# Two attentions written out unit by unit, with row maxima, their transfers and the stores of sums by halves of the queries

## The reference

```python
# biased: 16 heads of 8, a bias by distance added to the scores, no mask
att = jnp.einsum('bhqd,bhkd->bhqk', q, k) * (1.0 / math.sqrt(HS))
att = att + compute_bias(rel_emb, t, t)
att = jax.nn.softmax(att, axis=-1)
o = jnp.einsum('bhqk,bhkd->bhqd', att, v)
# causal: the same sizes, a mask in place of the bias
scores = jnp.where(causal, jnp.einsum("bhqd,bhkd->bhqk", q, k), neg)
attn = jax.nn.softmax(scores, axis=-1)
ctx = jnp.einsum("bhqk,bhkd->bhqd", attn, v)
```

## Time and profile before

| what | value |
|---|---|
| three runs, median (lowest to highest) | 2156.62 us (2148.72 to 2158.24) |
| the profiled execution, and its span | 2163.23 us, 2161.4 us |
| TensorE, VectorE, ScalarE, GpSimd busy, all of the span | 1726.3, 1528.8, 1183.4, 845.2 us |
| biased attention, first turn to last copy | 511 to 1224 us |
| causal attention, first turn to last copy | 1321 to 1831 us |

### The profile page before, as it was taken

One profiled execution on the slowest core, in us unless ns is written; L12 is line 12 of the kernel. 1 busy time (PEld: TensorE's weight loads), 2 busy tenths in 40 slices (PEclk: granted clock), 3 DMA queues, 4 the chain that ended last, 5 costly groups with the idle time before them and its releaser, 6 DMA issues. The chain is left out here.

```text
span 2161.4 us, 44387 instructions
## 1 busy us (share of the span) xinstructions
PE 1726.3 (80%) x14756; PEld 776.0 (36%) x14756; DVE 1528.8 (71%) x2661; ACT 1183.4 (55%) x2278; POOL 845.2 (39%) x1066
## 2 busy tenths in 40 slices
PE   5799999987899989989998536988988887600992
PEld 2666666652122222222222223333333332500772
DVE  4768888878899989989897177776777772570224
ACT  3222222232689878878888533676676776300332
POOL 1100000024477777777777533121111221156354
PEclk8799999997799999999999867898899997555996
DMA  2193000004001001001100315111111110401444
GB/s 77 60 138 78 0 0 0 0 12 140 15 21 35 19 20 37 19 20 27 28 19 5 79 26 154 27 37 24 33 37 37 35 24 14 126 33 55 124 138 139
DMA packets 93747, 103.32 MB, mean 48 GB/s; under 512 B 27137, under 2 KB 61649, under 8 KB 93041
## 3 DMA queue, kind: packets, MB, share of 16 engines
q1 hardware_dynamic: 89456, 92.33, 17.6%
q0 software_dynamic: 4096, 8.43, 1.1%
HBM read 63.65 MB, written 36.80 MB: 46 GB/s over the span
## 5 line engine op out<-in xcount | busy, mean ns | idle before, releaser
L1178 DVE TENSOR_REDUCE ba_at_top<-ps 128x2 f32<-128x1024 f32 x512 | 592.8, 1219 | 36.3 <-PE ps L1078 30.9
L1215 ACT ACTIVATE ba_at_ring<-ps 128x512 f32<-128x512 f32 x1024 | 556.6, 596 | 98.2 <-PE ps L1104 86.3
L1262 POOL TENSOR_TENSOR ba_at_ring<-ba_at_ring,rb_near 128x256 f32<-128x256 f32 (+2 forms) x640 | 480.0, 783 | 199.0 <-ACT ba_at_ring L1215 198.6
L1178 DVE TENSOR_REDUCE ca_at_top<-ps 128x2 f32<-128x1024 f32 (+3 forms) x384 | 352.7, 955 | 86.3 <-PE ps L1078 42.5
L1215 ACT ACTIVATE ca_at_ring<-ps 128x512 f32<-128x512 f32 (+3 forms) x768 | 335.5, 490 | 132.0 <-PE ps L1104 123.1
L1078 PE MATMUL ps<-kop,qop 48*128 48x512 bf16 (+3 forms) x1792 | 345.4, 386 | 65.4 <-DVE ba_at_top L1178 31.1
L1104 PE MATMUL ps<-qop,kop 49*128 49x512 bf16 (+3 forms) x1792 | 343.7, 380 | 60.5 <-DMA qop<-ca_at_negm 14.3
L1123 PE MATMUL ps<-ba_at_ring,ba_at_low 128*32 128x256 f32 (+2 forms) x4096 | 339.4, 405 | 18.1 <-ACT ba_at_osb L1200 15.6
L1104 PEld LDWEIGHTS ps<-qop,kop 49*128 49x128 bf16 x1792 | 86.7, 93 | 442.0 <-ACT ba_at_ring L1215 245.7
L1255 POOL TENSOR_SCALAR_AFFINE_SELECT ca_at_ring<-ca_at_ring 128x512 f32<-128x512 f32 x128 | 81.3, 636 | 417.5 <-ACT ca_at_ring L1215 417.5
L520 ACT ACTIVATE gm_sg<-ps,gm_bias 128x512 f32<-128x512 f32 x128 | 88.0, 687 | 236.3 <-PE ps L460 236.3
(11 more groups left out here) (316 smaller groups left out, 1696.3 us busy)
## 6 DMA issues: line engine op xcount, KB each, us to landing
cs_fc<-in_fc_w SPq DMA_DIRECT2D x32, 256.0 KB, 2.8
qk_parts<-ba_at_ring SPq DMA_DIRECT2D x24, 256.0 KB, 3.6
qop<-qk_parts SPq DMA_DIRECT2D x64, 96.0 KB
kop<-qk_parts SPq DMA_DIRECT2D x64, 96.0 KB
qk_parts<-ca_at_ring SPq DMA_DIRECT2D x24, 256.0 KB, 3.6
ex_xi<-expert_rows_in SPq DMA_DIRECT2D x16, 258.0 KB, 3.1
expert_rows_in<-gm_zero SPq DMA_DIRECT2D x1, 4096.0 KB
expert_rows_out<-gm_zero SPq DMA_DIRECT2D x1, 4096.0 KB
```

The source lines that it names most:

```text
L1178: nc.vector.tensor_reduce(top[:, k0 // CH, 2 * pair:2 * pair + 2, i], k.ps[:, slot:slot + 2, 0:k1 - k0], AX.X, ALU.max).then_inc(a_read, 1)
L1215: nc.scalar.activation(ring[:, t % RING, 0:q1 - q0], k.ps[:, B_BANK + bank_of(g, t), 0:q1 - q0], ACT.Exp).then_inc(exped, 1)
L1262: ins = nc.gpsimd.tensor_tensor(w, w, a.near[:, g * HG + j, lo - (i - 1) * P:hi - (i - 1) * P], ALU.mult)
```

## The change

Only `attend` is changed, for both attentions.

- The loop over batches is gone: all 16 units are written out on every engine, with constant semaphore targets.
- Row maxima are found by halves of the queries: first query tiles 0 to 3 (biased: 16 turns; causal: 8), then tiles 4 to 7 (16 each). Each half has its own join (causal: the second alone), transposition of 16 rows, negation, four DMAs of 4 x 128 elements, and a semaphore `mrow[g][half]`. The scores of a half wait for that half alone.
- All turns and transpositions of all units form one list, ITEMS. A transposition stands two turns behind the last turn of its half. `plan` gives each item a step, ahead of its use by a lead: the larger of two shares (first half's part of the turns; second half's part of the steps) plus AHEAD, 0.2 (biased) or 0.28 (causal). That makes 0.70 of a unit in the biased attention and 0.99 in the causal one. Before step 0 only unit 0's first half is worked off.
- The sums are stored by halves, each with its own semaphore; ScalarE's copy waits for the store of the same half a unit earlier.
- SyncE goes through the steps in one list: loads at step 0 of a unit, `largest` at the step of the transposition, `store` at fixed steps, and `invert` at step 6 of the last unit.

```diff
-    AHEAD = 0.17
-    GAP = 3
+    AHEAD = 0.28 if causal else 0.2
...
-    TILES = [0, 7, 1, 6, 2, 5, 3, 4]
+    TILES = ([0, 1, 2, 3], [4, 5, 6, 7])
...
+        for u in range(NU):
+            for half in range(2):
+                for t in turns_of(half):
+                    push((u, half, t))
+                due.append([2, (u, half, None)])
...
+        lead = max(sum(cost[:n0]) / sum(cost), 1 - begin1) + AHEAD
...
+                when = u - lead + sum(cost[:n]) / sum(cost)
...
+        early = [x for x in range(len(at)) if at[x] < 0 and x > turned_at[0, 0]]
+        room = first_of[1] * NPAIR - 1
+        for y, x in enumerate(early):
+            at[x] = y * room // len(early)
+        for x in range(1, len(at)):
+            if x > turned_at[0, 0]:
+                at[x] = max(at[x], at[x - 1], 0)
...
-        def units(eng, one):
-            one(0, 0)
-            with eng.Fori(0, B - 1) as b:
-                for g in range(1, NG):
-                    one(b, g)
-                one(b + 1, 0)
-            for g in range(1, NG):
-                one(B - 1, g)
...
+                def store(u, half):
+                    b, g = where(u)
+                    sp.wait_ge(o_copied, 2 * u + half + 1)
                     for j in range(HG):
+                        sp.dma_start(a.o[b, g * HG + j, :, half * CH:(half + 1) * CH],
+                                     osb[32 * j:32 * j + VA, half * CH:(half + 1) * CH]).then_inc(stored[half], 16)
...
+                for s in range(NU * NQ_ + (LAG + 1) * NPAIR):
+                    u, n = s // NQ_, s % NQ_ // NPAIR
+                    if s % NQ_ == 0 and u + 2 < NU:
+                        load(u + 2)
+                    for x in (STEPS[s] if s < len(STEPS) else ()):
+                        if ITEMS[x][2] is None:
+                            largest(*ITEMS[x][:2])
+                    if s % NPAIR == 0 and n == LAG and u:
+                        store(u - 1, 1)
+                    if s % NPAIR == 0 and n == last_of[0] + 1 + LAG:
+                        store(u, 0)
+                    if s == (NU - 1) * NQ_ + (LAG + 1) * NPAIR:
+                        invert()
...
+                    if n == first_of[half] and pair == 0:
+                        pe.wait_ge(mrow[g][half], (b + 1) * HG * 16)
...
+                for x in range(turned_at[0, 0] + 1):
+                    top_turn(x)
+                for u in range(NU):
+                    for n in range(NP_):
+                        owner, vn = (u, n - LAG) if n >= LAG else (u - 1, NP_ - LAG + n)
                         for pair in range(NPAIR):
+                            score_pair(u, n, pair)
+                            for x in STEPS[u * NQ_ + n * NPAIR + pair]:
+                                top_turn(x)
```

More of the change, by code:

```diff
@@ L856, in attend @@
     NBANK = 3
-    AHEAD = 0.17
-    GAP = 3
+    AHEAD = 0.28 if causal else 0.2
+    NU = B * NG
+    NPAIR = HG // 2
+    HB = CH // P
     def pieces():
-        order = ([0, 1, 2, 3, 4, 5, 6, 7],) * 2 if causal else ([1, 5, 2, 6, 0, 7, 3, 4], [3, 0, 6, 1, 5, 2, 7, 4])
+        if not causal:
+            order = ([1, 5, 2, 6, 0, 7, 3, 4], [3, 0, 6, 1, 5, 2, 7, 4])
+            return [(half, [(i, half * CH, (half + 1) * CH, 0)]) for half in range(2) for i in order[half]]
         out = []
         for half in range(2):
[L867 to L872, removed]
+            q1 = (half + 1) * CH
+            for i in range(HB * (half + 1)):
+                out.append((half, [(i, max(half * CH, i * P), q1, 0)]))
         return out
@@ L907, in top_keys @@
+    if causal:
+        NEARS = [n for n in range(NP_) if any(q0 == i * P for i, q0, q1, at in PIECES[n][1])]
+    else:
+        NEARS = [n for n in range(NP_) if near(n)]
     def top_keys(i):
         return (i + 1) * P if causal else L
[L910 to L935, removed]
-        return out
@@ L938, in attend, with turns_of, turn_list, push @@
-    NEARS = [n for n in range(NP_) if (PIECES[n][2] == PIECES[n][0] * P if causal else near(n))]
+    TILES = ([0, 1, 2, 3], [4, 5, 6, 7])
+    def turns_of(half):
+        return [(pair, i, k0, min(top_keys(i), k0 + CH)) for pair in range(NPAIR) for i in TILES[half]
+                for k0 in range(0, top_keys(i), CH)]
+    def turn_list():
+        out, due = [], []
+        def push(item):
+            out.append(item)
+            for d in due:
+                d[0] -= 1
+            while due and due[0][0] <= 0:
+                out.append(due.pop(0)[1])
+        for u in range(NU):
[3 more added lines that the diff above has]
+                due.append([2, (u, half, None)])
+        out.extend(d[1] for d in due)
+        return out
@@ L940, in attend @@
+    STEPS, ITEM_AT = plan()
     with ExitStack() as c:
@@ L1085, in add_mask @@
                     for part in range(2):
[L1086 to L1088 removed]
+                        for s in range(2):
+                            rows = slice(64 * s, 64 * s + 64)
+                            ins = nc.tensor.matmul(k.ps[:, slot + s, at:at + P], k.half[rows, part, 0, :], k.half[rows, part, 1, :],
@@ L1266, in _ @@
                 pool.wait_ge(vs_zero, 1)
-                values(0, 0)
-                units(pool, bias)
+                values(0)
+                for u in range(NU):
+                    for n in NEARS:
+                        if n == NEARS[len(NEARS) // 2]:
+                            next_values(u)
+                        if causal:
+                            select(u, n)
+                        else:
+                            weigh(u, n)
 def weight_sums(a, b):
```

352 lines of the change are left out of this document (168 added, 184 removed).

## The result

The changed kernel takes 2191.8 us (median of its runs) against 2155.5 us before: ratio 1.017, 95% interval 1.012 to 1.021. The other 18 us between the medians no trace shows; the other executions of the changed kernel had a mean granted clock of 0.865 or 0.866, the profiled one 0.873.

What follows compares the result with a forecast made beforehand. Biased units were taken as nearly level with VectorE ending last, causal ones as uneven, not full; 2163.2 - 23 (biased) - 25 (causal) = 2115 us for the profiled execution, 2110 for the median, 8-in-10 range 2078 to 2150.

Steps and rivals of the forecast that it cites:

- Biased start: Start of the biased attention: first scores 16 us earlier, most handed back in a longer unit 0; -4 us, bounds -10 to +8.
- Biased units 1 to 14: Biased units at VectorE's 39.1 us plus late maxima and clock drops: 39.9 instead of 41.65 us each, -24.5 us in all.
- Unit 15: Last biased unit: TensorE waits about 5 us for last maxima sent behind SyncE's inversion; +5.5 us, bounds +3 to +9.
- Causal start: Start of the causal attention: first scores 13 us earlier, unit 0 46 instead of 35.7 us; -3 us, bounds -9 to +6.
- Causal unit 15: Last causal unit: keeps its 30 us, as it had no turns before and has three now.
- Causal units 1 to 14: Causal units as today's straight unit, 28.2 instead of 29.75 us each: -22 us, bounds 27.0 (-38) and 30.5 (+10).
- rival 1: Both attentions: smooth order frees more, biased units at VectorE's 39.1 us, causal ones at 27; about 2077 us; 22%.
- Rival 2: Both attentions: waits only move, maxima late by 0.9 us at biased halves, 1.5 at causal second half; 2148 us; 13%.
- Rival 3: Causal units: second half's maxima late behind the loads, then lower clock; 5 us a unit, 2185 us, slower; 7%.
- Rival 4: All units: straight code stalls for its instructions, 3.58 us once a unit; 2218 us; 4%.

Runs made afterwards that it cites:

- experiment 7: The kernel of experiment 3 with the turns left over for unit 0 packed from step 0 on, biased and causal: 2089.7 us, 0.971 of the kernel before.
- experiment 8: The kernel of experiment 7 with SyncE's inversion issued behind the transfers of biased unit 15's last maxima: 2088.1 us, 0.970 of the kernel before.
- Experiment 2: The kernel before with only its Fori loops written out in both attentions; order, transfers and stores unchanged: 2127.5 us, 0.986 of the kernel before.
- experiment 3: The changed kernel, split by halves, with one causal turn in every step: 2106.4 us, 0.977 of the kernel before.
- experiment 9: The changed kernel with each causal transposition four turns behind its half's last turn instead of two, turns still bunched: 2138.9 us, 0.993 of the kernel before.
- 12: The kernel before, written out, unsplit, one causal turn a step, long and short alternating, transposition at step 18: 2092.1 us, 0.970 of the kernel before.
- 14: The kernel of 12 with a causal unit's 8 short turns first, then its 16 long ones: 2112.0 us, 0.979 of the kernel before.
- experiment 5: The changed kernel with the causal second half's turns one a step, the first half's still bunched: 2142.9 us, 0.996 of the kernel before.
- experiment 11: The changed kernel with one part of the causal mask added twice in each diagonal turn (512 more matmuls): 2163.4 us, 1.003 of the kernel before.

## Why the prediction was wrong

*Biased start, -4.* Measured: -3.5 (scores 17.3 earlier, unit 0 13.8 longer, with the thirteen turns in step 11). Right. But what I took as given there, experiment 7 showed to be 14.5 us for the taking (VectorE idles 4.0 to 5.6 us ahead of each of the few turns in steps 0 to 10, and then reduces eleven in one run of 12.5 us).

*Biased units 1 to 14, 39.9 us, -24.5.* Measured 40.46, -16.7. The mechanism was right (no branch, clock 1.00), the size was off by 0.56 us a unit. VectorE is busy 38.4 us [the first window above], as summed; 2.1 us of its idleness stay. The sum had the idleness at the transposition go, "since two turns are now already filled". It didn't: TensorE waits for the reduction ahead of each of the two transpositions (rows of the unit in that window), and VectorE then idles 1.8 us a unit for TensorE.

```profile
772.25 0.28 PE L1086 MATMUL ps<-cst,ba_at_top 128*16 128x128 f32 x1 [0.38 <-DVE ba_at_top L1183]
792.64 0.28 PE L1086 MATMUL ps<-cst,ba_at_top 128*16 128x128 f32 x1 [1.12 <-DVE ba_at_top L1183]
```

*Unit 15, +5.5.* Measured +3.0, and by another mechanism: experiment 8 took my wait away and gained nothing that can be told from noise.

*Causal start, -3.* Measured -0.2: 11.9 us gained, 11.7 given back. *Causal unit 15, no change.* Measured +2.1.

*Causal units 1 to 14, 28.2 us, -22.* This is **the step that failed**: 32.23 us, +34.7, above the upper bound of 30.5. Of the 66.4 us between the 2115 forecast for the profiled execution and the 2181.6 measured, this term makes 57 and the biased units 8. The prediction said "All branches go, so the straight unit of today, 28.2, is the nearest row", weighed transfers against VectorE's idleness and "set gain and loss equal" (with 4.2 us for the twelve loads, which its row gives as 4.4: late by 0.9, not 0.7, which changes nothing here, as none of these units waited for its maxima). Experiment 2 confirms the row for straight code in the old order (28.17). But the change also replaced the order, and I never set its causal steps against VectorE's 0.4 to 1.2 us a reduction, though I had done exactly that for the thirteen turns of unit 0. Two turns and a transposition beside empty steps cost 1.5 us in gaps and 2.56 in clock a unit, against the 28.17 us of the old order. My sentence "any unevenness of steps costs", an argument against rival 1, was the right one.

*Rivals.* Rival 1's 27 us a unit is what the split gives with an even order (experiment 3), but the changed kernel hasn't that order. Rival 2: no, the maxima are in time. Rival 3, the one that ended slower, foresaw 2185 for a wrong reason: a wait for causal maxima shows only ahead of unit 0, and its +5 us a unit, of which 4 came, arose from the waits for VectorE and the clock behind them. What it borrowed from the Trainium skill, *TensorE: Matmul & The Clock Gate*, section "HAM oscillation — how this bites in real kernels", was right in kind, recurring waits between bursts that bring the clock down anew; here waits of 0.5 to 0.9 us for VectorE did it, not for DMA. Rival 4: experiment 2 excludes it. The cost of small transfers that the Trainium skill names (*DMA: Bandwidth & Descriptors*, "Rules for kernel authors") shows no large effect here: the wait for the second half's maxima in experiment 3 is 0.29 us in the unit shown, and nothing separates the size of the transfers from their number or their place.

## What to carry to other kernels

When a change replaces the order in which one engine hands work to another, put the new order step by step against the duration of the receiver's work; a mean share of 80% says nothing when one step holds three items and the next none. An item that waits for the last result, not for the last but one, is best kept out of a full step (experiment 9), and behind a short piece of work rather than a long one (12 and 14). And where TensorE's short waits recur, price the clock too: here it cost 2.56 us a unit, as much as the gaps' 2.6.

## What the runs showed of the hardware

- The same instructions ran 28.5 us at clock 1.00 and 31.8 us at 0.84, in neighbouring units of one execution (experiment 5).
- More matmuls made a kernel faster: 512 on top gave 28 us between medians and 21 between the profiled executions, since the mean clock of the causal units rose from 0.88 to 0.96 (experiment 11).
- TensorE fell to 1.2 GHz behind waits as short as 0.5 to 0.9 us where these came in a row. The window from 1370 us, right behind steps 0 and 1 of causal unit 1, has a mean clock of 0.61. Longer waits that stood apart did not do it: the biased units 1 to 14 of the same execution wait 0.4 and 1.1 us and keep 1.00. Nor does the row of waits do it each time: four of the 14 causal units, with the same waits, keep 1.00.

```profile
1370.00:1383.00 13.00, 11.31 (x116) 4.33 (x116) 6.08 (x9) 6.25 (x17) 2.76 (x5) 0.61 0.21 46
```
